# A graph-attention megakernel: the adjacency ring of the attention loaded and counted by single blocks instead of five parts, with the first pair of units of each chunk written out ahead of its loop

## The chip, the core and the metric

The kernel runs on one core of a Trainium2 chip. The metric is the device time of one execution in microseconds (us). The core has five engines that run side by side and meet only at semaphores: TensorE (PE in the profile; its weight loads are PEld), VectorE (DVE), ScalarE (ACT), GpSimd (POOL) and SyncE (SP). SP computes nothing here; it issues all the DMA transfers of the kernel, one after the other, and waits in between for whatever each transfer needs.

## What is computed

Four graph layers run one after the other on x (3327 nodes, 128 features) and a dense adjacency matrix adj (3327 x 3327). Each layer is followed by a residual and a layer norm. Layers 0, 2 and 3 are graph convolutions of different kinds. The change lies in layer 1, an attention:

```
n, d = x.shape                      # 3327, 128
h = Wq.shape[0] // d                # 8
q = (x @ Wq.T).reshape(d, n, h)     # 128 "batches", each with 3327 rows of 8
k = (x @ Wk.T).reshape(d, n, h)
v = (x @ Wv.T).reshape(d, n, h)
a = einsum('dnh,dmh->dnm', q, k) * d ** -0.5
a = softmax(a + adj + adj, axis=2)  # adj is both spatial and edge encoding
out = einsum('dnm,dmh->dnh', a, v).reshape(n, h * d) @ Wo.T
```

So there are 128 batches of a 3327 x 3327 score matrix, and the same adjacency is added (twice) to each of them.

## The kernel before

**Chunks, units and blocks.** The 26 blocks of 128 query rows are split into four chunks, `CHUNKS = ((24, 2), (0, 8), (8, 8), (16, 8))` (first block, number of blocks). Chunk 0 has only two query blocks, and four batches are done side by side in it; chunks 1 to 3 have eight query blocks (1024 columns) and one batch at a time. One such piece of work is a *unit*: 32 units in chunk 0 and 128 in each of the others, 416 in all. A unit goes over the 26 key blocks j = 0 to 25, each a tile of 128 keys by 1024 query columns. All loops are over pairs of units (`Fori`), whose bodies are written out in full.

**What happens to a block.** TensorE computes the scores (L1097) into PSUM. For 18 of the blocks VectorE adds the adjacency (L1209, `added`) and ScalarE takes the exponential of two or three such blocks at once (L1170). For the other 8, `POOL_BLOCKS = (0, 3, 6, 9, 13, 16, 19, 22)`, ScalarE takes the exponential first (L1167) and GpSimd multiplies it by a prepared factor exp(2 adj) (L1183, `multiplied`). TensorE then weighs V with the result (L1117), some five to seven blocks later, and at block 9 of the next unit VectorE copies the finished sums out (`finish`, L1194). TensorE scores up to four blocks ahead; VectorE's blocks have two score places, GpSimd's one.

**The ring.** The adjacency (or factor) block j of a chunk has to lie in SBUF for all units of the chunk: 26 blocks of 128 x 1024 floats, 512 KB each (128 KB each in chunk 0). The ring `adj_ring` has 28 slots of a full block, `ADJ_SLOTS = BLOCKS + 2`. In chunks 1 to 3, block j of the next chunk goes into the slot that block j - 2 of this chunk has, and blocks 0 and 1 into the two spare slots. Chunk 0's small blocks lie from slot 21 on, and some of its keys in slots 13 to 20.

**Loading and counting by parts.** `ADJ_PARTS` cuts the 26 blocks into five parts, 0 to 5, 6 to 12, 13 to 16, 17 to 20 and 21 to 25, with one semaphore each (`ring.loaded[part]`). VectorE (L1203 to L1205) and GpSimd (L1180, L1181) wait at the first block of a part until all of the part has landed. They do this in every pair of units, as the wait stands in the loop's body. GpSimd waits only at those first blocks that are its own, 0 and 13.

**The changeover on SP.** Inside a chunk SP loads, per unit, keys and queries (`load`, L630, L637, L975), V (`load_v`, L984) and stores the sums (`store`, L1005). When a chunk c from 1 on ends, SP's order is: once the last unit but one is scored, `load(c + 1, 0, 0)` (keys and queries of the next chunk's first unit); five waits that the present chunk's ring has landed; `used`, which waits until the last unit has done block 3; ring part 0; V of the next chunk's first unit; a store; parts 1, 2 and 3, each behind a `used`; once the last unit is scored, keys and queries of the next chunk's second unit; part 4; its V; the last store. From chunk 0 to chunk 1 there is room for parts 0 and 1 already during chunk 0; part 2 comes when the last unit but one is scored, and parts 3 and 4, then the second unit's keys and queries, when the last one is.

Of the kernel before, what the change touches and what calls it, by code (L numbers as in the profile page):

```python
# [13 lines left out]
ALU = mybir.AluOpType  # L14
# [731 lines left out]
def bound_phase(nc, keep, q_norms, k_norms, top, flag, ring, k_tile):  # L746
# [3 lines left out]
    with ExitStack() as stack:  # L750
# [9 lines left out]
        @block.sync  # L760
        def _(sp):
            sp.dma_start(k_len[:, :], k_norms[0:BATCHES * N].rearrange("(d n) -> d n", n=N)).then_inc(k_loaded, LOAD)
            sp.dma_start(q_len[:, :], q_norms[0:BATCHES * N].rearrange("(d n) -> d n", n=N)).then_inc(q_loaded, LOAD)
            for part in range(len(ADJ_PARTS)):
                ring.load(sp, 0, part, True)
# [67 lines left out]
class AdjRing:  # L833
# [4 lines left out]
    def __init__(self, mem, adj_t, factors):  # L838
        self.adj_t, self.factors = adj_t, factors
        self.tile = mem.sb("adj_ring", [P, ADJ_SLOTS * WIDTH])  # L840
        self.loaded = mem.sems("adj_ring_loaded", len(ADJ_PARTS))
        self.part_of = [n for n, (begin, end) in enumerate(ADJ_PARTS) for _ in range(begin, end)]
# [7 lines left out]
    def load(self, sp, c, part, factored):  # L850
        first, nb = CHUNKS[c]
        for j in range(*ADJ_PARTS[part]):
            of = self.adj_t[first:first + nb, :, j, :]
            if factored and j in POOL_BLOCKS:
                of = self.factors[first:first + nb, :, POOL_BLOCKS.index(j), :]
            sp.dma_start(self.block(c, j).rearrange("p (i q) -> p i q", q=P), of.rearrange("i p q -> p i q")
                         ).then_inc(self.loaded[part], LOAD)

    def ready(self, c, part, factored):

        times = c + 1 if factored else c + 2
        return times * (ADJ_PARTS[part][1] - ADJ_PARTS[part][0]) * LOAD


def attention_phase(nc, keep, ring, k_tile, pool_blocks, k_parts, q_parts, q_shift, v_ext, o_rows):
# [45 lines left out]
    with ExitStack() as stack:  # L911
# [49 lines left out]
        def _(sp):  # L961
# [45 lines left out]
            def next_part(c, part):  # L1007
                ring.load(sp, c + 1, part, n_pool > 0)
# [4 lines left out]
            for part in range(len(ADJ_PARTS)):  # L1013
                sp.wait_ge(ring.loaded[part], ring.ready(0, part, True))
                if not n_pool:
                    ring.load(sp, 0, part, False)
                    sp.wait_ge(ring.loaded[part], ring.ready(0, part, False))
            for part in range(2):
                next_part(0, part)
            spare = ADJ_SLOTS - BLOCKS  # L1020
            for c in range(len(CHUNKS)):
# [16 lines left out]
                if more:  # L1038
                    all_scored(done - 1)
                    load(c + 1, 0, 0)  # L1040
                    if c:
                        for part in range(len(ADJ_PARTS)):
# [130 lines left out]
        def _(pool):  # L1173
            if n_pool:
# [580 lines left out]
```

## Time and profile before

| | |
|---|---|
| time of the runs | 11077.53 us (median of 3, 11073.33 to 11080.54) |
| span of the profiled execution | 11077.6 us; no other time is given for it |
| busy share in the span | ScalarE 93%, TensorE 90%, VectorE 89%, GpSimd 72% |
| mean granted TensorE clock | 0.982 of full |
| attention | first add at 713.1 us, last at 10526.7 us |
| changes of chunk | about 1490, 4484 and 7512 us |
| loads of the ring | 104, of which 26 in the small form |

The times in rows are microseconds from the start of the span, unless marked ns. In a timeline, a row with xN stands for N instructions of one kind in a row, the second number is the time from the start of the first to the end of the last, and the square brackets hold the idle time of the engine before it and what ended it. For a DMA on SP's queue the second number is the time that the issue took; the landing, when all its data is in place, comes later and is listed by itself as microseconds from issue to landing (least, median, most). PEclk is TensorE's granted clock as a share of the full 2.4 GHz. TensorE's busy time is modelled.

### The profile page before, as it was taken

The numbers are of one execution on the slowest core, as the hardware profiler recorded it, in microseconds if no ns is written. First come the engines' busy times: TensorE is split into PE (matmuls) and PEld (weight loads), VectorE is DVE, ScalarE is ACT, GpSimd is POOL, SyncE is SP. The second block draws the span as 40 slices with busy tenths as digits, with TensorE's granted clock in tenths as the row PEclk, the third lists the DMA queues.
The fourth block names the chain that finished last, engine by engine and source line by source line (L and its number), as shares of the span: only waits on it lengthen the run. The fifth ranks groups of instructions, "written<-read, shape, count | busy, mean of one in ns | idle before, by whom it ended". The sixth has DMA issues, their size and how long they took to land. (4 is left out here: it accounts for less than half of the span.)

```text
span 11077.6 us, 307002 instructions
## 1 busy us (share of the span) xinstructions
PE 9989.2 (90%) x115286; PEld 4513.5 (41%) x115286; DVE 9834.5 (89%) x9022; ACT 10277.8 (93%) x7161; POOL 7988.9 (72%) x3346
## 2 busy tenths in 40 slices
PE   5859999999999999899999999998999999999988
PEld 5525543333333333333333333333333333333383
DVE  7469989999999999899999999998999999999958
ACT  3559999999999999999999999999999999999916
POOL 0038878888888888788888888887888888888800
PEclk8979999999999999999999999999999999999999
DMA  9997743333333332433333333335332333333264
GB/s 389 319 226 101 100 84 50 50 49 48 48 50 50 50 49 48 94 50 49 48 48 50 50 50 49 48 48 95 50 49 48 49 50 50 49 49 47 46 209 176
DMA packets 426842, 902.84 MB, mean 82 GB/s; under 512 B 86887, under 2 KB 349038, under 8 KB 379790
## 3 DMA queue, kind: packets, MB, share of 16 engines
q1 hardware_dynamic: 426732, 901.33, 40.5%
q8 instruction: 74, 1.21, 0.0%
q14 instruction: 36, 0.29, 0.0%
HBM read 745.35 MB, written 155.64 MB: 81 GB/s over the span
## 5 line engine op out<-in xcount | busy, mean ns | idle before, releaser
L1209 DVE SCALAR_TENSOR_TENSOR a_probs<-ps,adj_ring 128x1024 f32<-128x1024 f32 x7488 | 8855.1, 1220 | 777.3 <-PE ps L1097 633.4
L1183 POOL TENSOR_TENSOR a_pool_probs<-a_pool_probs,adj_ring 128x1024 f32<-128x1024 f32 x3328 | 7972.6, 2396 | 1884.3 <-ACT a_pool_probs L1167 1877.7
L1170 ACT ACTIVATE a_probs<-a_probs 128x2048 f32<-128x2048 f32 (+1 forms) x3328 | 8701.1, 2615 | 42.9 <-DVE a_probs L1209 42.7
L1167 ACT ACTIVATE a_pool_probs<-ps 128x1024 f32<-128x1024 f32 x3328 | 5012.0, 1506 | 49.1 <-PE ps L1097 49.1
L1097 PE MATMUL ps<-a_q,a_k 34*128 34x512 f32 (+1 forms) x21632 | 4091.5, 445 | 806.5 <-ACT a_pool_probs L1167 614.6
L1117 PE MATMUL ps<-a_probs,a_v 128*9 128x256 f32 x59904 | 3860.2, 380 | 0.0
L1097 PEld LDWEIGHTS ps<-a_q,a_k 34*128 34x128 f32 x21632 | 1794.5, 185 | 3477.0 <-ACT a_pool_probs L1167 1631.1
L1117 PEld LDWEIGHTS ps<-a_probs,a_v 128*9 128x9 f32 x59904 | 1579.3, 91 | 1602.0 <-issue 201.4
L1117 PE MATMUL ps<-a_pool_probs,a_v 128*9 128x256 f32 x26624 | 2068.1, 382 | 1.5 <-POOL a_pool_probs L1183 1.5
L1117 PEld LDWEIGHTS ps<-a_pool_probs,a_v 128*9 128x9 f32 x26624 | 395.4, 88 | 974.2 <-issue 937.6
L602 POOL MEMSET v_rows<- 128x512 f32 x2 | 1.9, 1038 | 403.6 <-POOLq L90 403.6
L1097 PE MATMUL ps<-a_q,adj_ring 34*128 34x256 f32 x1664 | 222.4, 280 | 0.0
L1627 POOL MEMSET e_nat<- 128x1 f32 x3 | 0.2, 98 | 300.3 <-POOLq L90 300.3
L1194 DVE COPY a_o<-ps 128x256 f32<-128x256 f32 x417 | 177.0, 424 | 30.1 <-PE ps L1117 5.2
L296 ACT ACTIVATE tr<-ps 128x1664 f32<-128x1664 f32 x52 | 78.4, 1555 | 134.2 <-DMA adj_t<-tr 124.3
L272 PE MATMUL ps<-ident,nat 128*128 128x128 f32 x676 | 108.2, 334 | 99.2 <-ACT tr L296 91.4
L796 POOL MEMSET a_k<- 128x3328 f32 x2 | 5.7, 2872 | 245.4 <-POOLq L90 245.4
L416 PE MATMUL ps<-g0z,g0tile 128*128 128x128 f32 x1352 | 155.7, 277 | 9.4 <-DVE g0z L467 9.4
L1097 PEld LDWEIGHTS ps<-a_q,adj_ring 34*128 34x128 f32 x1664 | 161.1, 190 | 0.0
L1590 PE MATMUL ps<-e_both,e_h 128*128 128x512 f32 (+2 forms) x364 | 152.1, 569 | 7.1 <-DVE e_both L1650 7.1
L416 PEld LDWEIGHTS ps<-g0z,g0tile 128*128 128x128 f32 x1352 | 154.4, 194 | 9.5 <-issue 9.5
L1445 PE MATMUL ps<-g2z,g2tile 128*128 128x128 f32 x1352 | 155.1, 277 | 1.3 <-PEq L90 1.3
(174 smaller groups left out, 2177.6 us busy)
## 6 DMA issues: line engine op xcount, KB each, us to landing
a_k<-k_parts SPq DMA_DIRECT2D x1664, 208.0 KB
a_q<-q_parts SPq DMA_DIRECT2D x3072, 16.0 KB
a_v<-v_ext SPq DMA_DIRECT2D x384, 117.0 KB, 2.1
adj_t<-tr SPq DMA_DIRECT2D x26, 1664.0 KB, 20.7
g0tile<-adj_t SPq DMA_DIRECT2D x26, 1664.0 KB, 9.6
g2tile<-adj_t SPq DMA_DIRECT2D x26, 1664.0 KB
nat<-in_adj SPq DMA_DIRECT2D x25, 1663.5 KB, 18.8
e_nat<-in_adj SPq DMA_DIRECT2D x25, 1663.5 KB, 7.0
```

Of the source, the lines that this page charges most:

```text
L272: ins = nc.tensor.transpose(ps[:, col:col + P], nat[b][:, P * j:P * (j + 1)], keep.ident[:, :])
L296: nc.scalar.activation(tr[b][:, HALF * P * h:HALF * P * (h + 1)], ps[:, half * h:half * h + HALF * P], ACT.Copy).then_inc(copied[h], 1)
L416: ins = nc.tensor.matmul(acc[i % ACC_BUFS], layer.tile[b][:, j, :], z[:, j, :], start=j == 0, stop=j == BLOCKS - 1)
L1097: ins = nc.tensor.matmul(ps[:, at:at + half], keys[b][n][row:row + SCORE_ROWS, P * j:P * (j + 1)].bitcast(F32R), q_tile[b][row:row + SCORE ...
L1117: ins = nc.tensor.matmul(acc[b][32 * g:32 * g + VG, :], v_tile[b][0:rows_of[j], 3 - g if several else 0, j, :], p[:, SHARE * g:SHARE * (g ...
L1167: nc.scalar.activation(probs(k), score(j), ACT.Exp, scale=SCALE).then_inc(scores_exped, 1)
L1170: nc.scalar.activation(sums_of(k), sums_of(k), ACT.Exp, scale=2.0).then_inc(sums_exped, 1)
L1183: nc.gpsimd.tensor_tensor(beside(c, probs(k)), beside(c, probs(k)), adj_of(c, j), ALU.mult).then_inc(multiplied, 1)
L1194: v.tensor_copy(o_tile[b][:, :], acc[b]).then_inc(acc_read, 1)
L1209: v.scalar_tensor_tensor(out=beside(c, probs(k)), in0=beside(c, score(j)), scalar=SCALE / 2, in1=adj_of(c, j), op0=ALU.mult, op1=ALU.add). ...
L1445: ins = nc.tensor.matmul(acc[i % ACC_BUFS], second.tile[b][:, j, :], second.z[:, j, :], start=j == 0, stop=j == BLOCKS - 1)
L1590: ins = nc.tensor.matmul(ps[:, at:to], h[0:rows, i, :], both[i % 2][0:rows, at:to], start=begin and to < NP, stop=end, skip_group_check=True)
```

## The change

Ring blocks are loaded, counted and waited for one by one. There are 26 semaphores in place of five. `next_blocks(c, js)` issues blocks one at a time and, from chunk 1 on, puts before block j a wait that block j - 2 of the last unit is done (`used(c, j - spare)`, now one wait, on the engine that works on that block); blocks 0 and 1 have no such wait. The cuts in SP's order are moved: 13 blocks (in place of 6) before V of the next chunk's first unit, and 24 (in place of 21) before the keys and queries of its second unit. VectorE and GpSimd wait for each of their blocks in the first unit of a chunk only; for that the first pair of units of each chunk is written out ahead of the loop, and the loop has no waits for the ring. In the changeover from chunk 0 the order of the transfers is as before.

```diff
-ADJ_PARTS = ((0, 6), (6, 13), (13, 17), (17, 21), (21, BLOCKS))
+VALUES_FROM, KEYS_FROM = 13, 24
...
-        self.loaded = mem.sems("adj_ring_loaded", len(ADJ_PARTS))
+        self.loaded = mem.sems("adj_ring_loaded", BLOCKS)
...
-            def used(c, upto):
-                j, done = upto - 1, units_before[c + 1] - 1
-                sp.wait_ge(added, done * n_dve + dve_rank[j] + (not by_pool[j]))
-                if n_pool:
-                    sp.wait_ge(multiplied, done * n_pool + pool_rank[j] + by_pool[j])
+            def used(c, j):
+                done = units_before[c + 1] - 1
+                if by_pool[j]:
+                    sp.wait_ge(multiplied, done * n_pool + pool_rank[j] + 1)
+                else:
+                    sp.wait_ge(added, done * n_dve + dve_rank[j] + 1)
...
-            def next_part(c, part):
-                ring.load(sp, c + 1, part, n_pool > 0)
+            def next_blocks(c, js):
+                for j in js:
+                    if c and j >= spare:
+                        used(c, j - spare)
+                    ring.load(sp, c + 1, j, n_pool > 0)
...
                     if c:
-                        for part in range(len(ADJ_PARTS)):
-                            sp.wait_ge(ring.loaded[part], ring.ready(c, part, n_pool > 0))
-                        used(c, ADJ_PARTS[0][1] - spare)
-                        next_part(c, 0)
+                        for j in range(BLOCKS):
+                            sp.wait_ge(ring.loaded[j], ring.ready(c, n_pool > 0))
+                        next_blocks(c, range(VALUES_FROM))
                     else:
-                        next_part(c, 2)
+                        next_blocks(c, range(*KEYS_AT))
                     sp.wait_ge(batch_summed, done - 1)
                     load_v(c + 1, v_of_unit(c + 1, 0), 0)
                 sp.wait_ge(stored[1], (done // 2 - 1) * per_store)
                 store(c, done, last - 1, 0)
                 if more:
                     if c:
-                        for part in (1, 2, 3):
-                            used(c, ADJ_PARTS[part][1] - spare)
-                            next_part(c, part)
-                    all_scored(done)
-                    if c:
+                        next_blocks(c, range(VALUES_FROM, KEYS_FROM))
+                        all_scored(done)
                         load(c + 1, 1, 1)
-                        used(c, ADJ_PARTS[4][1] - spare)
-                        next_part(c, 4)
+                        next_blocks(c, range(KEYS_FROM, BLOCKS))
                     else:
-                        next_part(c, 3)
-                        used(c, BLOCKS)
-                        next_part(c, 4)
+                        all_scored(done)
+                        next_blocks(c, range(KEYS_AT[1], FEW_AT))
+                        if n_pool:
+                            used(c, pool_blocks[-1])
+                        used(c, BLOCKS - 1)
+                        next_blocks(c, range(FEW_AT, BLOCKS))
                         load(c + 1, 1, 1)
...
+            def add(c, pair, first):
+                for k in range(units):
+                    b, j = divmod(k, BLOCKS)
+                    unit = pair * 2 + b
+                    if not by_pool[j]:
+                        if first and b == 0:
+                            dve.wait_ge(ring.loaded[j], ring.ready(c, n_pool > 0))
...
-                with dve.Fori(units_before[c] // 2, units_before[c + 1] // 2) as pair:
...
+                begin, end = units_before[c] // 2, units_before[c + 1] // 2
+                add(c, begin, True)
+                with dve.Fori(begin + 1, end) as pair:
+                    add(c, pair, False)
```

GpSimd's `multiply(c, pair, first)` is built in the same way around L1183.

## Rows read from the trace of the kernel before

**Rows 1.** Busy time by stretch: us, engines' busy us (instructions), PEclk, DMA share, GB/s.

```profile
1550.00:4400.00 2850.00, 2648.72 (x31638) 1093.91 (x31634) 2642.90 (x2314) 2850.00 (x1948) 2332.22 (x974) 1.00 0.31 49
1490.00:1516.00 26.00, 22.05 (x202) 8.63 (x196) 16.67 (x15) 18.96 (x13) 15.40 (x7) 0.74 0.48 72
4484.00:4540.00 56.00, 35.18 (x298) 13.26 (x294) 26.35 (x25) 28.55 (x19) 22.48 (x10) 0.70 0.86 184
7512.00:7564.00 52.00, 30.94 (x292) 11.62 (x292) 26.05 (x24) 25.80 (x18) 20.11 (x10) 0.77 0.92 189
```

**Rows 2.** VectorE's timeline, chunk 1 to 2: start, us, engine, line, operands [idle before].

```profile
4437.38 0.42 DVE L1194 COPY a_o<-ps 128x256 f32<-128x256 f32 x1
...
4449.70 8.41 DVE L1209 SCALAR_TENSOR_TENSOR a_probs<-ps,adj_ring 128x1024 f32<-128x1024 f32 x7 [0.69 <-PE ps L1097]
...
4460.80 0.42 DVE L1194 COPY a_o<-ps 128x256 f32<-128x256 f32 x1
...
4521.53 3.49 DVE L1209 SCALAR_TENSOR_TENSOR a_probs<-ps,adj_ring 128x1024 f32<-128x1024 f32 x3 [9.63 <-DMA adj_ring<-adj_t]
...
4537.18 0.41 DVE L1194 COPY a_o<-ps 128x256 f32<-128x256 f32 x1
```

**Rows 3.** Landings of ring loads issued at 4506.08 (first), 4512.7 and 4514.5.

```profile
DMA to landing us min/median/max: 9.6/9.6/9.6
...
L856 SPq DMA_DIRECT2D adj_ring<-adj_t x2: 1639/1680/1720, 4512.7 to 4514.5; - x2
...
DMA to landing us min/median/max: 6.9/7.0/7.0
```

**Rows 4.** The sync queue's timeline, chunk 1 to 2.

```profile
4456.79 0.26 SPq L975 DMA_DIRECT2D a_q<-q_shift  x1
4462.81 0.39 SPq L856 DMA_DIRECT2D adj_ring<-factors  x1
...
4470.49 1.73 SPq L984 DMA_DIRECT2D a_v<-v_ext  x1
```

**Rows 5.** GpSimd's timeline, last unit of chunk 1.

```profile
4460.33 2.39 POOL L1183 TENSOR_TENSOR a_pool_probs<-a_pool_probs,adj_ring 128x1024 f32<-128x1024 f32 x1 [0.31 <-ACT a_pool_probs L1167]
```

**Rows 6.** Busy time by stretch, just before the ring's loads.

```profile
4458.50:4459.00 0.50, 0.50 (x10) 0.18 (x2) 0.50 (x1) 0.50 (x2) 0.50 (x1) 1.00 0.01 0
```

**Rows 7.** The sync queue's timeline at the start of attention.

```profile
715.53 0.40 SPq L986 DMA_DIRECT2D a_v<-v_ext  x1
716.11 0.39 SPq L856 DMA_DIRECT2D adj_ring<-factors  x1
```

**Rows 8.** The sync queue's and VectorE's timelines, chunk 2 to 3.

```profile
7483.24 0.25 SPq L975 DMA_DIRECT2D a_q<-q_shift  x1
7489.27 0.39 SPq L856 DMA_DIRECT2D adj_ring<-factors  x1
...
7547.48 3.49 DVE L1209 SCALAR_TENSOR_TENSOR a_probs<-ps,adj_ring 128x1024 f32<-128x1024 f32 x3 [12.14 <-DMA adj_ring<-adj_t]
...
7561.17 0.42 DVE L1194 COPY a_o<-ps 128x256 f32<-128x256 f32 x1
```

**Rows 9.** Busy time by stretch, a restart (the last figures are clock, DMA, GB/s).

```profile
1494.00:1506.00 12.00, 11.43 (x86) 4.21 (x86) 7.48 (x7) 8.21 (x5) 4.81 (x3) 0.50 0.58 87
```

**Rows 10.** VectorE's timeline, few-blocks chunk to chunk 1.

```profile
1488.01 1.23 DVE L1209 SCALAR_TENSOR_TENSOR a_probs<-ps,adj_ring 128x1024 f32<-128x1024 f32 x1 [0.26 <-PE ps L1097]
1493.29 3.48 DVE L1209 SCALAR_TENSOR_TENSOR a_probs<-ps,adj_ring 128x1024 f32<-128x1024 f32 x3 [4.05 <-DMA adj_ring<-adj_t]
...
1510.72 0.41 DVE L1194 COPY a_o<-ps 128x256 f32<-128x256 f32 x1
```

**Rows 11.** Landings of ring loads issued at 1479.3 and 1481.1.

```profile
DMA to landing us min/median/max: 8.5/10.3/12.0
```

**Rows 12.** DMA issues of the page: count, KB each, median us to landing.

```profile
a_v<-v_ext SPq DMA_DIRECT2D x384, 117.0 KB, 2.1
```

**Rows 13.** DMA queues from 4600 to 7400: packets, MB, share.

```profile
q1 hardware_dynamic: 57576, 137.57, 31.4%
```

More of the change, by code:

```diff
@@ L848, in block, with load, ready @@
         return self.tile[:, at:at + width]
-    def load(self, sp, c, part, factored):
+    def load(self, sp, c, j, factored):
         first, nb = CHUNKS[c]
[L852 to L862, printed above, removed]
+        of = self.adj_t[first:first + nb, :, j, :]
+        if factored and j in POOL_BLOCKS:
+            of = self.factors[first:first + nb, :, POOL_BLOCKS.index(j), :]
+        sp.dma_start(self.block(c, j).rearrange("p (i q) -> p i q", q=P), of.rearrange("i p q -> p i q")
+                     ).then_inc(self.loaded[j], LOAD)
+    def ready(self, c, factored):
+        return (c + 1 if factored else c + 2) * LOAD
 def attention_phase(nc, keep, ring, k_tile, pool_blocks, k_parts, q_parts, q_shift, v_ext, o_rows):
@@ L1012, in _ @@
                 load_v(0, v_of_unit(0, b), b)
-            for part in range(len(ADJ_PARTS)):
-                sp.wait_ge(ring.loaded[part], ring.ready(0, part, True))
+            for j in range(BLOCKS):
+                sp.wait_ge(ring.loaded[j], ring.ready(0, True))
                 if not n_pool:
[L1016 to L1019, printed above, removed]
+                    ring.load(sp, 0, j, False)
+                    sp.wait_ge(ring.loaded[j], ring.ready(0, False))
             spare = ADJ_SLOTS - BLOCKS
+            next_blocks(0, range(KEYS_AT[0]))
             for c in range(len(CHUNKS)):
@@ L1194, in finish @@
                 v.tensor_copy(o_tile[b][:, :], acc[b]).then_inc(acc_read, 1)
+            def add(c, pair, first):
+                for k in range(units):
+                    b, j = divmod(k, BLOCKS)
+                    unit = pair * 2 + b
+                    if not by_pool[j]:
+                        if first and b == 0:
+                            dve.wait_ge(ring.loaded[j], ring.ready(c, n_pool > 0))
+                        dve.wait_ge(scores_ready[False], unit * n_dve + (dve_rank[j] + 1))
+                        v.scalar_tensor_tensor(
+                            out=beside(c, probs(k)), in0=beside(c, score(j)), scalar=SCALE / 2, in1=adj_of(c, j),
+                            op0=ALU.mult, op1=ALU.add).then_inc(added, 1)
+                    if j == FINISH_AT:
+                        finish(1 - b, unit)
             v.memset(ps[:, BANK * 6:], 1.0).then_inc(cleared, 1)
@@ L1198, in _ @@
             for c in range(len(CHUNKS)):
-                with dve.Fori(units_before[c] // 2, units_before[c + 1] // 2) as pair:
-                    for k in range(units):
-                        b, j = divmod(k, BLOCKS)
-                        unit = pair * 2 + b
-                        if b == 0 and j in (begin for begin, _ in ADJ_PARTS):
-                            part = ring.part_of[j]
-                            dve.wait_ge(ring.loaded[part], ring.ready(c, part, n_pool > 0))
-                        if not by_pool[j]:
-                            dve.wait_ge(scores_ready[False], unit * n_dve + (dve_rank[j] + 1))
-                            v.scalar_tensor_tensor(
-                                out=beside(c, probs(k)), in0=beside(c, score(j)), scalar=SCALE / 2, in1=adj_of(c, j),
-                                op0=ALU.mult, op1=ALU.add).then_inc(added, 1)
-                        if j == FINISH_AT:
-                            finish(1 - b, unit)
+                begin, end = units_before[c] // 2, units_before[c + 1] // 2
+                add(c, begin, True)
+                with dve.Fori(begin + 1, end) as pair:
+                    add(c, pair, False)
             dve.wait_ge(stored[1], (units_before[-1] // 2 - 1) * per_store)
```

23 lines of the change are left out of this document (11 added, 12 removed).

## The prediction

> **What bounds the kernel now.** I read the views in this order: busy time by stretch, the timelines of VectorE, GpSimd and the sync queue around the three changes of chunk, and the landings of the ring's loads. The reader is to see first that inside a chunk ScalarE is busy without a gap [rows 1]: it sets the pace, and one unit takes 4460.80 - 4437.38 = 23.42 us from one copy of the sums (L1194) to the next [rows 2]. Speeding another engine up there changes nothing. Time is lost only where a chunk ends. There ScalarE is idle for 26 - 18.96 = 7.0 us (few-blocks chunk to chunk 1), 56 - 28.55 = 27.5 us (1 to 2) and 52 - 25.80 = 26.2 us (2 to 3) [rows 1]. These 60.7 us, 0.55% of the span, are all that the change can work on.
>
> Why they are lost: 26 blocks of 512 KB have to arrive, and with the queue full SP gets rid of one only every 4514.5 - 4512.7 = 1.8 us [rows 3], while a unit uses one every 23.42 / 26 = 0.90 us. Two ring slots are spare; every other load waits until the last unit has freed a slot. So the end of a changeover is set by the landing of the last block, plus what must be done after it.
>
> **Where the ring's loads start.** Before, SP is through with the next chunk's keys and queries at 4456.79 + 0.26 = 4457.05, then sits until 4462.81 [rows 4]: it waits for block 3 of the last unit, the GpSimd multiply that starts at 4460.33 and runs 2.39 us [rows 5]. Meanwhile the DMA engines fall to nothing [rows 6]. After, blocks 0 and 1 need no slot of that unit. SP first passes 26 waits in place of 5. Five such waits cost it 716.11 - 715.53 - 0.40 = 0.18 us at the start of attention [rows 7], 0.036 us each, so 26 cost 0.9 us: first issue at 4458.0. Block 2 waits for block 0's multiply, which ended at 4460.33 - 0.31 = 4460.02 [rows 5]; the two blocks ahead of it keep the engines busy for 3.6 us, so they do not run dry. Block 5 waits for block 3 (4462.7), and its turn at that pace comes only at about 4467. Start shift: 4462.81 - 4458.0 = 4.8 us. From 2 to 3 it is the same: 7483.24 + 0.25 + 0.9 = 7484.4 against 7489.27, 4.9 us [rows 8]. Bounds: 5.7 if the waits cost nothing; 0 if the loads only pile up behind each other.
>
> **Where they end.** The same bytes go through the same queue. Before, unit 1's keys and queries go behind block 20; after, behind block 23. The second issue behind them (block 22 before, at 4506.08) lands 9.6 us later [rows 3]. After, that place is block 25's, 3 x 1.8 = 5.4 us later for the three blocks put ahead and 4.8 us earlier for the start: issued 4506.7, landed 4516.3. Before, block 25 was issued at 4514.5 and landed 6.9 us later, at 4521.4 [rows 3]. So the last landing moves 5.1 us earlier from 1 to 2; I take 4.9 from 2 to 3 (7547.4, just ahead of VectorE's start at 7547.48 [rows 8], becomes 7542.5).
>
> **What is left after it.** Before, VectorE could not touch block 21 until all of blocks 21 to 25 had landed; then it had blocks 21, 23, 24, 25 and six of the next unit to do before the copy. After, only 25 and those six. In the steady stretch add 21 starts at 4449.70 - 0.69 - 1.22 = 4447.8 and add 25 at 4452.1 [rows 2]: to the copy at 4460.80 that is 13.0 and 8.7 us. So 4.3 us of work move ahead of the last landing, into time in which VectorE idled. The restart is not at steady pace, as TensorE comes back at a granted clock of 0.50, 1.2 GHz [rows 9]. From VectorE's start on block 21 to the copy it took 15.6 us (4521.53 to 4537.18) [rows 2], 13.7 us (7547.48 to 7561.17) [rows 8] and 17.4 us (1493.29 to 1510.72) [rows 10]: 2.6, 0.7 and 4.4 us over 13.0, on average 2.6. After, VectorE works block by block, but keys and queries still hold it up for some 5 us just ahead of block 24, so the clock can fall again. I take the average, 2.6. Lower bound 0. Upper bound, all at the low level: TensorE's matmuls fill 2648.72 / 2850 of the time at full clock [rows 1], 0.84 us a block. The seven scorings to the copy need 5.9 us at full and 11.8 at half clock, with 2.7 for the first weighing and 1.0 for the last add 15.5 in all: 6.8 over the 8.7.
>
> A page bears on this. The Trainium skill, "TensorE: Matmul & The Clock Gate", section "Part 1: The HAM clock gate", holds that TensorE is throttled by default and that activity releases it. The trace agrees: 0.50 in the restarts. By that rule a changeover whose holes are short would keep 2.4 GHz, and the 2.6 us would go; the sum would be 5.2 us better.
>
> **Sum.** 1 to 2: the copy comes at 4516.3 + 8.7 + 2.6 = 4527.6 instead of 4537.18: 9.6 us. 2 to 3: 7542.5 + 11.3 = 7553.8 instead of 7561.17: 7.4 us. Few blocks to chunk 1: there the loads are issued in the same order at the same times. VectorE stood still from 1488.01 + 1.23 = 1489.24 to 1493.29 before block 21 [rows 10], for block 25 alone, issued at 1481.1 and landed 12.0 us later; block 24 had landed at 1479.3 + 8.5 = 1487.8 [rows 11]. After, it does 21, 23, 24 and wants 25 at 1492.9: 0.4 us of stall and no cold restart. Of ScalarE's 7.0 us I leave 0.8: 6.2 us gained (bounds 3 and 7.0). Start of attention: 21 more waits on SP, 0.8 us, ahead of a queue that soon is full; I charge 0.3 us (0 to 0.8).
>
> At no cost: the waits gone from VectorE's and GpSimd's loops (ScalarE has no gap there). V of the new chunk's first unit goes behind 13 blocks in place of 6: seven blocks are 12.7 us and the start 4.8 less, so it is issued at 4470.49 + 7.9 = 4478.4 [rows 4] and, at the 6.9 us of a ring load, there by 4485.3; TensorE wants it at about 4460.80 + 23.42 = 4484.2. What it loses is hidden by the wait for the blocks past 15; without that cover it would be 1 to 2 us. The store behind it is wanted only a unit later. The 21 added semaphores are cleared with the others at the phase's end. The longer straight code has to be loaded: today's chunk heads show no hole on VectorE but for the ring and TensorE [rows 2].
>
> 9.6 + 7.4 + 6.2 - 0.3 = 22.9 us. The profiled execution's span is 11077.6 us, with nothing listed around it, and the median of the runs is 11077.53, the same. Forecast: 11077.6 - 22.9 = 11054.7 us, 0.21% less.
>
> **Rivals.**
> A, *the drain takes the start back*: the last landing is no earlier, because keys and queries hold the queue up for longer when three more blocks are ahead of them. Left: 4.5 and 2.5 us of tail, 6.2 and -0.3: 12.9 us, 11064.7. For it: a block right behind them needs 9.6 us where another needs 6.9 [rows 3]. Against: the engines stand empty before the ring's loads today [rows 6], and the bytes are the same. Chance 0.15.
> B, *cold to the copy*: TensorE stays at 1.2 GHz all the way, 4.2 us more in each of two restarts: 14.5 us gained, 11063.1. For it: it stayed there for 12 us in one restart [rows 9]. Against: in the shortest it cost 0.7 us in all. Chance 0.14.
> C, *never cold*: work block by block keeps the clock up, 2.6 us less twice, and the full 5.7 us of start: 29.9 us, 11047.7. It is what the page above would give. Against: the hole before block 24. Chance 0.12.
> D, *slower: loops that fetch their code again*: the pair in front moves each loop body of VectorE and GpSimd to another address. If one body lay so that each pass had to fetch, the 63 passes of a chunk would each pay a transfer, 2.1 us as V's in quiet stretches [rows 12], less VectorE's slack of 2 x 0.7 us a pair (ScalarE's 23.42 against 18 x 1.22 + 0.42 + 0.3): 63 x 0.7 = 44 us, 11099 with the rest as summed. It decides from 22.9 / 63 = 0.36 us a pass. Against: today 2800 us of looping show no packet but the kernel's own queue's [rows 13]. The Trainium skill, "Runtime: NRT & Kernel Launch", section "Instruction fetch mechanics", says that a taken branch to a place outside the fetched pages forces a fetch first; by the same rows no loop here does so yet. Chance 0.04.
>
> **How the numbers follow.** My sum has 0.55. Its own range, from the restart (0.7 to 4.4 each) and the start (3 to 5.7), is 11049 to 11062. A and B reach to 11065, C to 11048, A and B together to 11073. Range 11046 to 11069: D and the worst combination stay outside, under 2 in 10. A difference of 0.2% (22 us) is about what can be told from no change. That line is 11055.4, so close to the forecast that the sum falls on its faster side 6 times in 10, 0.33; with C 0.12 and 0.03 for gains I do not see, 0.48. Slower by over 0.2%: 0.04. The rest, 0.48, is within.
>
> **What the new profile would show.** Right: ring loads issued about 1 us after the queries of the next chunk, no empty DMA stretch there; VectorE's waits for the ring split into short ones from about block 15 on; ScalarE idle about 1, 18 and 19 us in place of 7.0, 27.5 and 26.2; 23.42 us a unit elsewhere. Wrong: a last landing at the old distance from the old chunk's end (A); over 5 us lost between add 25 and the steady pace (B); none lost (C); instruction packets or a longer unit inside a chunk (D); TensorE waiting for a_v or a_q, the moved transfers not hidden.

## The result, and the profile after

The changed kernel takes 11060.68 us (median of 20 runs, 11054.0 to 11069.0) against 11077.7 us (20 runs, 11070.68 to 11081.78): the ratio is 0.9986, with a 95% interval of 0.9979 to 0.9992. That is 17.0 us less where 22.9 were forecast, inside the range, and by 0.14% on the "within 0.2%" side of the line. The profiled execution has a span of 11062.8 us, 14.8 less than that of before. The attention starts 1.75 us later in it (first add at 714.83 instead of 713.08) and is itself about 17 us shorter, from that add to its last copy of the sums.

One correction to the text on the kernel before: GpSimd's waits for the ring stand at blocks 0, 6 and 13, as block 6 too is its own and the first of a part. No number hangs on it.

Busy time by stretch comes first, for the same places as in [rows 1], shifted by as much as the last unit's copy has moved (+1.26, -0.98 and -6.66 us); then the steady stretch. Columns are as there.

```profile
1491.26:1517.26 26.00, 22.91 (x230) 9.02 (x222) 18.30 (x17) 20.62 (x14) 16.67 (x7) 0.80 0.46 74
4483.02:4539.02 56.00, 40.03 (x360) 15.16 (x356) 30.40 (x28) 33.77 (x23) 26.42 (x12) 0.73 0.82 167
7505.34:7557.34 52.00, 37.09 (x380) 14.41 (x384) 31.09 (x28) 34.27 (x24) 26.83 (x12) 0.80 0.84 171
...
1550.00:4400.00 2850.00, 2648.76 (x31640) 1093.70 (x31642) 2644.31 (x2314) 2850.00 (x1948) 2330.29 (x974) 1.00 0.31 49
```

ScalarE's idle time is now 5.4, 22.2 and 17.7 us in place of 7.0, 27.5 and 26.2 [rows 1]; forecast were about 1, 18 and 19. That is 1.7, 5.2 and 8.5 us less in place of about 6, 9.5 and 7. The steady stretch is what it was, to 0.04 us of TensorE: nothing was gained or lost inside a chunk. So the reading of where the time can be was right, and the first changeover is where the forecast missed by most.

VectorE's timeline, chunk 1 to 2 in the kernel after (it answers to [rows 2]):

```profile
4459.82 0.42 DVE L1197 COPY a_o<-ps 128x256 f32<-128x256 f32 x1
...
4483.23 0.42 DVE L1197 COPY a_o<-ps 128x256 f32<-128x256 f32 x1
...
4499.41 1.23 DVE L1207 SCALAR_TENSOR_TENSOR a_probs<-ps,adj_ring 128x1024 f32<-128x1024 f32 x1 [2.39 <-DMA adj_ring<-adj_t]
4501.23 1.23 DVE L1207 SCALAR_TENSOR_TENSOR a_probs<-ps,adj_ring 128x1024 f32<-128x1024 f32 x1 [0.59 <-DMA adj_ring<-adj_t]
4506.89 1.23 DVE L1207 SCALAR_TENSOR_TENSOR a_probs<-ps,adj_ring 128x1024 f32<-128x1024 f32 x1 [4.43 <-DMA adj_ring<-adj_t]
4515.75 1.23 DVE L1207 SCALAR_TENSOR_TENSOR a_probs<-ps,adj_ring 128x1024 f32<-128x1024 f32 x1 [7.64 <-DMA adj_ring<-adj_t]
4517.38 2.36 DVE L1207 SCALAR_TENSOR_TENSOR a_probs<-ps,adj_ring 128x1024 f32<-128x1024 f32 x2 [0.41 <-DMA adj_ring<-adj_t]
...
4530.59 0.42 DVE L1197 COPY a_o<-ps 128x256 f32<-128x256 f32 x1 [1.29 <-PE ps L1115]
```

Before, VectorE waited once for five blocks; now it works each block as it lands (4499.41 to 4506.89), stands still for the hole that the second unit's keys and queries tear (7.64 us before block 24 at 4515.75), and has only block 25 (4517.38) and what follows ahead of the copy. Measured from the old unit's copy (4460.80 before, 4459.82 now), VectorE gets its last block 57.6 us later, against 60.7 before. Forecast was a landing 5.1 us earlier; it is 3.2.

The sync queue in the same place (it answers to [rows 4]), and under it how long after issue the first ring load, and blocks 24 and 25, landed:

```profile
4455.82 0.25 SPq L972 DMA_DIRECT2D a_q<-q_shift  x1
4456.93 0.40 SPq L854 DMA_DIRECT2D adj_ring<-factors  x1
...
4505.98 0.25 SPq L972 DMA_DIRECT2D a_q<-q_shift  x1
4506.28 1.02 SPq L854 DMA_DIRECT2D adj_ring<-adj_t  x2
```

```profile
DMA to landing us min/median/max: 5.7/5.7/5.7
...
DMA to landing us min/median/max: 9.4/10.0/10.6
```

The 26 waits take 4456.93 - 4455.82 - 0.25 = 0.86 us (0.9 forecast), and the ring starts 4.90 us earlier against the old unit's copy (4.8 forecast). But block 0 now lands 5.7 us after its issue. Before, on empty engines, it was 4.1:

```profile
L856 SPq DMA_DIRECT2D adj_ring<-factors x1: 393/393/393, 4462.8 to 4462.8; - x1
...
DMA to landing us min/median/max: 4.1/4.1/4.1
```

The engines move 128 GB/s in 4457 to 4461, just behind the keys and queries, and 282 once the ring has them to itself. The reading is that the tail of the keys and queries is still arriving. It fits all the rows at hand: 5.7 us in the other changeover of this kernel too (issued at 7477.7), and 4.1 us again in experiment 4 for a first ring load that goes out ahead of the keys (at 4439.1).

```profile
4457.00:4461.00 4.00, 4.00 (x52) 1.59 (x52) 3.47 (x5) 4.00 (x4) 3.68 (x2) 1.00 0.88 128
...
4459.00:4483.00 24.00, 22.34 (x276) 9.14 (x268) 22.24 (x20) 24.00 (x18) 19.32 (x10) 1.00 1.21 282
```

Few-blocks chunk to chunk 1, VectorE and then TensorE (it answers to [rows 10]):

```profile
1492.40 3.61 DVE L1207 SCALAR_TENSOR_TENSOR a_probs<-ps,adj_ring 128x1024 f32<-128x1024 f32 x3 [0.69 <-PE ps L1095]
1498.15 1.23 DVE L1207 SCALAR_TENSOR_TENSOR a_probs<-ps,adj_ring 128x1024 f32<-128x1024 f32 x1 [2.14 <-PE ps L1095]
...
1509.82 0.42 DVE L1197 COPY a_o<-ps 128x256 f32<-128x256 f32 x1 [1.27 <-PE ps L1115]
```

```profile
1493.93 0.73 PE L1095 MATMUL ps<-a_q,a_k 34*128 34x512 f32 x4
1497.61 0.50 PE L1095 MATMUL ps<-a_q,a_k 34*128 34x512 f32 x2 [2.94 <-DMA a_q<-q_shift]
```

The wait for the ring is gone, as forecast. In its place TensorE waits 2.94 us for the second unit's keys and queries, which stand behind block 25 in the queue. It comes back at 2.4 GHz, falls to 1.2 GHz within two microseconds, and works at that without a gap until about 1509.5:

```profile
1498.00:1499.00 1.00, 1.00 (x22) 0.53 (x24) 0.85 (x1) 1.00 (x1) 1.00 (x1) 1.00 0.00 0
1499.00:1500.00 1.00, 1.00 (x14) 0.34 (x8) 0.37 (x1) 0.25 (x1) 0.11 (x1) 0.58 0.78 200
...
1499.50:1509.00 9.50, 9.50 (x70) 3.54 (x70) 5.94 (x5) 5.65 (x4) 4.74 (x2) 0.50 0.69 104
```

**What is added up below.** The *excess* of a changeover is the sum of the distances from copy to copy across it, less 23.42 us each. Before it was 7.8, 28.8 and 27.1 us; after, 5.8, 23.4 and 18.7. The *restart* is the time from VectorE's start on block 25 to the copy in that unit; in the steady stretch it is 8.7 us. Both are read from one profile of each kernel; the clock, as will be seen, moves them by some us from one changeover to the next.

### The profile page after: what moved, and what is told of

The parts are those of the page before. It is cut to its first block and busy times, and to the rows that moved or that the text cites. A ratio compares the mean times of both kernels' runs of the same rounds, so it can differ in the third digit from the quotient of the medians.

```text
span 11062.8 us, 306459 instructions
## 1 busy us (share of the span) xinstructions
PE 9991.2 (90%) x115286; PEld 4517.4 (41%) x115286; DVE 9840.4 (89%) x9022; ACT 10276.4 (93%) x7161; POOL 7981.3 (72%) x3346
```

## The experiments

Nine kernels. Each is set against runs of the kernel before on the same chip: 11077.54 us for the first four, 11074.91 for the next four and 11074.31 for the last. Each differs from the kernel after by what its diff shows, except the second, which starts from the kernel before.

**1. The waits alone.** The cuts and the gate of before are put back; blocks are loaded and waited for one by one.

```diff
-VALUES_FROM, KEYS_FROM = 13, 24
+VALUES_FROM, KEYS_FROM = 6, 21
...
+                        used(c, 3)
                         next_blocks(c, range(VALUES_FROM))
```

> The changed kernel with the order and the gate of before: ring loads start behind block 3 of the last unit, V behind block 5, the second unit's keys behind block 20; only the counting and waiting are by single blocks. Theory (two separate parts: the start of the loads moves the last landing, the waits move 4.3 us of adds ahead of it): last landing as before (60.6 us after the old chunk's last copy from 1 to 2, 60.2 from 2 to 3), changeovers 2 to 4 us shorter each from 1 to 2 and 2 to 3, and 2.0 us from chunk 0 to 1 as in the changed kernel; in all 6 to 10 us less than before, 11068 to 11072. Rival (the single waits are the whole gain): as the changed kernel, 11061. Rival (the waits gain nothing without the start): 11076 to 11078.

Measured: 11066.39 us (11059.69 to 11078.7), ratio 0.9990 [0.9981, 0.9999]: 11.1 us faster than before. Excess 3.8, 21.8 and 22.7. VectorE gets block 25 60.4 and 60.5 us after the old copy, as before (60.7, 60.2): without the early start the last landing does not move. This kernel's gain lies behind that landing: 4.3 us of adds in each of two changeovers are done ahead of it. Its profile is of the fastest of its runs (11059.69) and shows more than that, as its restart from 1 to 2, 8.2 us, is 3.1 us nearer to the steady pace than it was before.

**2. The early start alone.** From the kernel before: part 0 is cut in two, and its first two blocks need no slot.

```diff
-ADJ_PARTS = ((0, 6), (6, 13), (13, 17), (17, 21), (21, BLOCKS))
+ADJ_PARTS = ((0, 2), (2, 6), (6, 13), (13, 17), (17, 21), (21, BLOCKS))
...
-                        used(c, ADJ_PARTS[0][1] - spare)
                         next_part(c, 0)
+                        used(c, ADJ_PARTS[1][1] - spare)
+                        next_part(c, 1)
```

> The kernel before with its first part cut into blocks 0 and 1 (issued at once) and 2 to 5 (behind block 3's use); waits by part everywhere. Theory: the last landing moves 3 us earlier in the changeovers 1 to 2 and 2 to 3, as in the changed kernel (it moved 3.1 and 3.3 there), the adds behind it stay; 6 us less than before, 11071 to 11073, nothing from chunk 0 to 1. Rival (the start gains nothing, the gates hold the later blocks up): 11077 to 11079.

Measured: 11073.25 us (11062.51 to 11077.97), ratio 0.9995 [0.9986, 1.0004]. By itself the early start is worth 4.3 us, and the interval takes in nothing. The profile says more: VectorE's last ring wait ends 56.7 and 56.1 us after the old copy, 4.0 and 4.2 earlier than before. So rival A is wrong, the start is not taken back in the drain. But its 8.2 us in the landings are not all seen in the median, and this profile is of the fastest of the kernel's runs (11062.51). It also has an excess of only 4.5 us from chunk 0 to 1, where this kernel does just what the kernel before does and that had 7.8: VectorE waits for block 25 in both (3.78 and 4.05 us), but TensorE then runs at 1.2 GHz for 3.4 us here and for 13.7 there. Together the two parts give 11.1 + 4.3 = 15.4 of the 17.0 us.

**3. The cuts of before.** All of the change, but with V and the second unit's keys where they were.

```diff
-VALUES_FROM, KEYS_FROM = 13, 24
+VALUES_FROM, KEYS_FROM = 6, 21
```

> The changed kernel with V behind block 5 and the second unit's keys and queries behind block 20, as before. Theory (bytes are conserved, the place of the keys only moves the hole): last landing within 1 us of the changed kernel's, time within 3 us of it, 11058 to 11064. Rival (the hole just before block 24 is what lets TensorE's clock fall): the restart costs under 1 us in both, 4 to 6 us less than the changed kernel, 11055 to 11057. Rival (the later cuts are what gained): 5 us more, 11066.

Measured: 11058.6 us (11056.03 to 11066.63), ratio 0.9985 [0.9976, 0.9994]: 18.9 us faster than before. Excess 5.3, 19.0 and 19.9; block 25 at 57.2 and 56.9. The moved cuts bring nothing that can be told from zero.

**4. The spare blocks first.** The waits and blocks 0 and 1 go ahead of the next chunk's first keys.

```diff
-                    all_scored(done - 1)
-                    load(c + 1, 0, 0)
                     if c:
                         for j in range(BLOCKS):
                             sp.wait_ge(ring.loaded[j], ring.ready(c, n_pool > 0))
-                        next_blocks(c, range(VALUES_FROM))
+                        next_blocks(c, range(spare))
+                    all_scored(done - 1)
+                    load(c + 1, 0, 0)
+                    if c:
+                        next_blocks(c, range(spare, VALUES_FROM))
```

> The changed kernel with ring blocks 0 and 1 (spare slots) and the 26 waits issued ahead of the next chunk's first keys and queries, in a stretch where the DMA engines are idle. Theory (the drain of 26 blocks is bound by bytes and ends the changeover): 2 x 1.8 us of transfer leave the drain and the loads no longer start into the tail of the keys; the last landing moves 4 to 5 us earlier in each of two changeovers, 8 to 10 us less than the changed kernel, 11051 to 11053. Rival (the gates on the last unit's blocks set the pace of the first loads): block 2's gate keeps the rest where it is, under 2 us less, 11059 to 11061.

Measured: 11056.22 us (11048.71 to 11057.88), ratio 0.9979 [0.9970, 0.9988]: 21.3 us faster than before. VectorE gets block 25 52.6 and 52.1 us after the old copy:

```profile
4459.05 0.42 DVE L1199 COPY a_o<-ps 128x256 f32<-128x256 f32 x1
...
4511.64 2.36 DVE L1209 SCALAR_TENSOR_TENSOR a_probs<-ps,adj_ring 128x1024 f32<-128x1024 f32 x2 [0.44 <-DMA adj_ring<-adj_t]
...
4523.15 0.41 DVE L1199 COPY a_o<-ps 128x256 f32<-128x256 f32 x1
```

That is 4.9 us earlier than in the kernel after (57.6), and 4.8 in the other changeover: 3.6 are the two blocks at 1.8 us, and the rest is near the 1.6 us of the overlap with the tail of the keys. What counts is how early the engines have ring loads to themselves. Of the 9.7 us the restarts took some back, 11.5 and 12.9 us to the copy against 8.7 at full pace, and the medians show 4.3 us more than for the kernel after.

**5. From the few-blocks chunk, slots one by one.** A small block of chunk 0 lies in a quarter of a slot; blocks 21 to 24 of chunk 1 are issued as soon as the four small ones in their slot are done, instead of behind the last unit's scores. The second unit's keys and queries, behind them, come earlier too.

```diff
+                        for n in range(4):
+                            few = range(4 * n, 4 * n + 4)
+                            used(c, max(j for j in few if not by_pool[j]))
+                            if n_pool:
+                                used(c, max(j for j in few if by_pool[j]))
+                            next_blocks(c, (FEW_AT + n,))
                         all_scored(done)
                         next_blocks(c, range(KEYS_AT[1], FEW_AT))
...
-                        next_blocks(c, range(FEW_AT, BLOCKS))
+                        next_blocks(c, (BLOCKS - 1,))
```

> The changed kernel; in the changeover from chunk 0 alone, blocks 21 to 24 of chunk 1 are issued slot by slot as the last unit of chunk 0 frees its small blocks, in the stretch before that unit is all scored, where the DMA engines are idle; 17 to 20, 25 and the keys follow as before. Theory (what was left of that changeover, 5.8 us over the steady pace, comes from the second unit's keys and queries, which TensorE waited for until 1497.6): four blocks of 1.8 us leave the queue ahead of them, they land about 7 us earlier and the wait of TensorE for a_q is gone; the changeover costs under 1 us over steady and the time is 4 to 6 us less than the changed kernel's, 11055 to 11057. Rival (the landing of block 25 or the gates on slots delay it all the same): changeover still 3 us or more, 11060.

Measured: 11054.78 us (11051.6 to 11060.24), ratio 0.9981 [0.9972, 0.9990]: 20.1 us faster than before. The changeover has gone; its excess is nil:

```profile
1475.60 2.20 SPq L630 DMA_DIRECT2D a_k<-k_parts  x2
```

The same load in the kernel after:

```profile
1485.50 2.18 SPq L630 DMA_DIRECT2D a_k<-k_parts  x2
```

VectorE's copies in this experiment:

```profile
1477.63 0.42 DVE L1203 COPY a_o<-ps 128x256 f32<-128x256 f32 x1
...
1501.05 0.42 DVE L1203 COPY a_o<-ps 128x256 f32<-128x256 f32 x1
...
1524.47 0.42 DVE L1203 COPY a_o<-ps 128x256 f32<-128x256 f32 x1
```

The second unit's keys start 2 us before the old unit's copy, where the kernel after starts them 5.5 us behind it (1485.50 against 1479.99). With them in time TensorE does not wait, and the clock stays: 1.00 in all of 1480 to 1530. The other two changeovers are as in the kernel after (18.9 and 21.1). By the medians, experiment 5 gains 3.1 us on the kernel after.

**6. Small keys.** In the last two changeovers the second unit of a new chunk loads only 128 columns of its keys; the rest of that buffer keeps old keys, so this unit computes something else and the kernel is a measurement only. This leaves out some 800 KB behind block 23.

```diff
-            def load(c, d, b):
+            def load(c, d, b, short=False):
...
-                        load_k(sp, k_to, row, k_of[batch], sem)
+                        if short:
+                            load_k(sp, k_to[:, 0:P], row, k_of[batch][:, 0:P], sem)
+                        else:
+                            load_k(sp, k_to, row, k_of[batch], sem)
...
-                        load(c + 1, 1, 1)
+                        load(c + 1, 1, 1, True)
```

> The changed kernel, but in the changeovers 1 to 2 and 2 to 3 the keys of the second unit are loaded for the first 128 of 3328 columns only (the same number of transfers, 32 KB in place of 832 KB; the rest of that unit's keys are left stale, so its part of the output is other work). Theory (the 8.9 us between the landings of blocks 23 and 24 are the keys' transfer, bound by their bytes on few rows): the hole shrinks to 2 to 4 us, the last landing moves 5 to 6 us earlier in each, 10 to 12 us less than the changed kernel, 11049 to 11051. Rival (the hole is SP's time to issue the 14 transfers, 6 us): the last landing moves by under 2 us, 11057 to 11061.

Measured: 11048.62 us (11044.07 to 11054.09), ratio 0.9976 [0.9965, 0.9986]. The hole shrinks but stays:

```profile
4504.51 1.22 DVE L1210 SCALAR_TENSOR_TENSOR a_probs<-ps,adj_ring 128x1024 f32<-128x1024 f32 x1 [2.97 <-DMA adj_ring<-adj_t]
4509.02 1.23 DVE L1210 SCALAR_TENSOR_TENSOR a_probs<-ps,adj_ring 128x1024 f32<-128x1024 f32 x1 [3.29 <-DMA adj_ring<-adj_t]
4510.82 2.36 DVE L1210 SCALAR_TENSOR_TENSOR a_probs<-ps,adj_ring 128x1024 f32<-128x1024 f32 x2 [0.57 <-DMA adj_ring<-adj_t]
```

From block 23 to block 24 it is 4.5 us in place of 8.9. Block 25 comes 51.9 us after the old copy in place of 57.6, and both restarts are short (9.4 and 9.5 us). 4.4 us for some 800 KB are about 180 GB/s, an estimate, against 282 for the ring; why these bytes cost more is not shown. Of the 4.5 us that are left, 1.8 are the ring block itself; the rest fits the issuing of the 14 transfers, which takes SP from 4498.70 to 4505.04.

**7. No pair in front.** The waits stand in the loops' bodies again.

```diff
-                    multiply(c, begin, True)
-                    with pool.Fori(begin + 1, end) as pair:
-                        multiply(c, pair, False)
+                    with pool.Fori(begin, end) as pair:
+                        multiply(c, pair, True)
...
-                add(c, begin, True)
-                with dve.Fori(begin + 1, end) as pair:
-                    add(c, pair, False)
+                with dve.Fori(begin, end) as pair:
+                    add(c, pair, True)
```

> The changed kernel without the pair in front: the waits by block stand in the loops, 18 on VectorE and 8 on GpSimd in each pair of units. Theory (ScalarE sets the pace inside a chunk and a passed wait costs some 0.04 us of a slack of 0.7 us a unit): 23.42 us a unit and the changed kernel's time within noise, 11058 to 11064. Rival (the pair in front is worth something, as 18 waits take VectorE's slack): 18 x 0.04 = 0.7 us a pair, just at the slack; if it were over it by 0.1 us a pair, 19 us more, 11080.

Measured: 11059.48 us (11057.03 to 11062.68), ratio 0.9986 [0.9977, 0.9995], the ratio of the kernel after. The pair in front is worth nothing and costs nothing.

**8. Both early starts, keys behind block 15.** Experiments 4 and 5 together, and the second unit's keys moved forward.

```diff
-VALUES_FROM, KEYS_FROM = 13, 24
+VALUES_FROM, KEYS_FROM = 13, 16
...
```

> The two early issues together (spare blocks ahead of the next chunk's first keys, and chunk 0's slots as they come free), and the second unit's keys behind block 15 in place of 23. Theory (the three changeovers are separate, bytes are conserved, and the hole that the keys make does no harm where it stands far from the last landing): 9 us as from the spare blocks alone, 5 us of the chunk 0 changeover, and a restart under 1 us over steady in place of 3 to 4: 11044 to 11049. Rival (with the hole moved, blocks 16 on come late and the clock falls there as well): restart unchanged, 11050 to 11053.

Measured: 11046.83 us (11039.77 to 11050.4), ratio 0.9973 [0.9962, 0.9983]: 28.1 us faster than before. Excess nil, 14.7 and 18.4. The same kernel shows both kinds of restart. In chunk 1 to 2 it took 9.2 us, in 2 to 3 12.9, with these rows of busy time by stretch, each from about where block 25 is added:

```profile
4510.00:4520.00 10.00, 9.72 (x122) 4.02 (x123) 9.66 (x10) 9.96 (x8) 7.18 (x3) 1.00 0.57 84
...
7520.00:7530.00 10.00, 10.00 (x74) 3.52 (x70) 6.39 (x6) 7.77 (x5) 4.61 (x2) 0.50 0.70 100
```

In the one TensorE is back at 2.4 GHz, in the other it works ten microseconds without a gap at 1.2 GHz.

**9. The same with the cut of after.** Only `KEYS_FROM` differs from 8: it is 24.

```diff
-VALUES_FROM, KEYS_FROM = 13, 16
+VALUES_FROM, KEYS_FROM = 13, 24
```

> The change with both early starts (26 waits and blocks 0 and 1 ahead of the next chunk's first keys; from chunk 0 on the small blocks 21 to 24 issued one by one as their slots come free), the cuts left at 13 and 24. It differs from the last kernel only in where the second unit's keys and queries stand: behind block 23, not behind block 15. Theory: the queue is bound by its bytes, so the last landing stays where it is, 52 to 53 us behind the old unit's copy; but the hole of some 8 us now stands just before block 24, so TensorE restarts at 1.2 GHz and the restart costs 2.8 to 4.2 us as in the kernel with the spare blocks first, where it cost about 0.5: some 3 us more in each of two changeovers, a median 5 us above 11046.8, with 11050 to 11054 as its range, and an excess of 16 to 18 us in each of the last two changeovers. Rival: where the hole stands is worth nothing and the run comes out within 2 us of 11046.8. Second rival: the last kernel loses something by the early keys (they wait for all scores of the old unit, and the ring behind them stops), and this one is 3 us or more faster than it.

Measured: 11048.24 us (11040.84 to 11056.72), ratio 0.9975 [0.9966, 0.9984]. It is 26.1 us faster than before, 8 is 28.1. The first rival is the nearest: by the medians the place of the hole is worth 2 us, which these intervals don't tell from nothing. In the two profiles the excess is 36.3 against 33.1 us over the last two changeovers, but the restarts are 13.2 and 11.5 here and 9.2 and 12.9 there, so they do not go with the place of the hole.

Beside each other (us; the difference is that of the medians, the excess is from one profile each; block 25 is counted from the old unit's copy; in 2 it is block 21, and it restarts from there, at 13.0 in the steady stretch):

| kernel | difference | excess 0-1, 1-2, 2-3 | block 25 | restart |
|---|---|---|---|---|
| after | -17.0 | 5.8, 23.4, 18.7 | 57.6, 56.9 | 13.2, 9.4 |
| 1 waits | -11.1 | 3.8, 21.8, 22.7 | 60.4, 60.5 | 8.2, 9.7 |
| 2 start | -4.3 | 4.5, 23.6, 23.0 | 56.7, 56.1 | 13.6, 13.8 |
| 3 old cuts | -18.9 | 5.3, 19.0, 19.9 | 57.2, 56.9 | 9.3, 10.6 |
| 4 spare first | -21.3 | 3.5, 16.5, 17.6 | 52.6, 52.1 | 11.5, 12.9 |
| 5 few slots | -20.1 | 0, 18.9, 21.1 | 57.2, 57.2 | 9.3, 11.5 |
| 6 small keys | -26.3 | 3.7, 13.7, 13.6 | 51.9, 51.7 | 9.4, 9.5 |
| 7 no pair | -15.4 | 4.9, 20.8, 19.6 | 56.8, 57.8 | 11.5, 9.5 |
| 8 both early | -28.1 | 0, 14.7, 18.4 | 53.1, 52.9 | 9.2, 12.9 |
| 9 both, cut 24 | -26.1 | 0, 19.8, 16.5 | 54.0, 52.5 | 13.2, 11.5 |

The last column goes with the clock. From VectorE's start on block 25, the granted clock is back at 2.4 GHz after 2.7 to 3.9 us wherever the restart is 9.2 to 9.7 us (experiment 2 aside, whose count starts at block 21), after 7.7 to 8.6 where it is 10.6 to 11.5, and after 12.2 to 12.8 where it is 12.9 to 13.2; in the one restart of 8.2 us it is back before. The excess from chunk 0 to 1 does the same. The kernel after and experiments 1, 3, 4, 6 and 7 have the same orders from chunk 0 to 1, and TensorE waits 2.9 to 3.6 us for the second unit's queries in all of them. Where it then runs at 1.2 GHz for 3.4 us the excess is 3.5 to 3.8 (1, 4 and 6), for 6.8 us it is 4.9 and 5.3 (7 and 3), and for 10.2 us 5.8 (after).

## Why the prediction was right, and where it was too high

**The bound.** Right. The steady stretch did not move, and all of the gain is in the changeovers.

**Start of the ring's loads.** Right: 4.90 and 4.92 us earlier against 4.8 and 4.9; 26 waits took 0.86 us.

**Last landing.** Right in kind, too large in size: the term of the sum that was mis-sized. It is 3.2 and 3.4 us earlier instead of 5.1 and 4.9. Two numbers explain the first. Block 25 was put on the queue at 4506.7, the time forecast, but the old unit's copy had moved 1.0 us forward, so it is 1.0 late in the frame of the changeover; and it landed 10.6 us after its issue, not 9.6. The first goes with block 0's 5.7 us instead of 4.1: with the early loads in the tail of the next chunk's first keys, up to 1.6 of the 4.9 us are spent before the ring runs at its pace. Why the second took 10.6 us no run settles. The forecast counted the stretch from issue to issue and took the engines to be free. Experiment 4, which puts those loads ahead of the keys, gets 4.8 to 4.9 us more; experiment 6 shows that the same queue is also shorter when bytes behind block 23 are left out. Rival A, that the drain takes all of it back, fell with this profile and with experiment 2, but about a third of the start is taken back.

**Work ahead of the last landing.** Right. Only block 25 and the next unit's six are left; with the landing where it was, experiment 1 is 11.1 us faster, against two times 4.3 and what the first changeover gives.

**The restart.** Forecast 2.6 us in each. In the kernel after it is 13.2 - 8.7 = 4.5 and 0.7 us, 2.6 on average, and over the six changeovers of the kernels after, 5 and 7, which run the same orders there, 2.0. That the average is just the forecast's 2.6 is luck, as its size is not fixed: rivals B (cold to the copy) and C (never cold) each describe single changeovers, not the kernel, and B was priced too high, at 6.8 us where a restart that is cold almost to the copy costs 4.5. Experiment 8 has 0.5 and 4.2 in one execution. What the rows show is that the clock falls twice, once well before the hole and once in it. In the kernel after, chunk 1 to 2:

```profile
4484.00:4492.00 8.00, 6.65 (x88) 2.96 (x88) 5.96 (x5) 7.97 (x7) 6.03 (x4) 1.00 1.20 296
4492.00:4494.00 2.00, 0.43 (x4) 0.07 (x2) 0.01 (x1) 2.00 (x2) 2.00 (x1) 1.00 1.22 290
4494.00:4496.00 2.00, 0.73 (x10) 0.30 (x10) 1.42 (x2) 0.55 (x1) 1.64 (x2) 1.00 1.22 290
4496.00:4498.00 2.00, 1.36 (x14) 0.42 (x10) 1.03 (x1) 0.94 (x1) 1.05 (x1) 0.51 1.22 290
...
4504.00:4506.00 2.00, 2.00 (x22) 0.56 (x14) 0.00 (x0) 0.40 (x1) 0.85 (x1) 0.50 1.29 167
4506.00:4508.00 2.00, 0.57 (x2) 0.19 (x2) 1.11 (x1) 1.02 (x1) 0.21 (x1) 0.93 0.79 110
4508.00:4510.00 2.00, 0.50 (x2) 0.19 (x2) 0.11 (x1) 0.00 (x0) 2.00 (x1) 0.93 1.11 147
4510.00:4512.00 2.00, 0.00 (x0) 0.00 (x0) 0.00 (x0) 0.00 (x0) 0.13 (x1) 0.50 0.98 104
...
4508.70:4517.00 8.30, 0.00 (x0) 0.00 (x0) 1.23 (x1) 0.00 (x0) 1.43 (x1) 0.56 1.00 171
4517.00:4529.00 12.00, 11.97 (x84) 4.33 (x88) 7.99 (x7) 8.41 (x5) 4.31 (x2) 0.50 0.57 84
```

Once the blocks come at the ring's pace, 1.8 us each, TensorE is busy for 1.16 of the 4 us up to 4496 and drops from 2.4 to 1.2 GHz; busy again, it is back at 2.4 from about 4506.3; and in the hole, in which it has no work, it drops once more at about 4510. After the hole it works without a gap at 1.2 GHz until about 4530. From 2 to 3 it goes the same way (down at 7517, back at 7527, down at 7530.5, back at 7541). So the restart begins at 1.2 GHz because of the second fall, and there the forecast's hole is borne out; the fall ahead of it, at the pace of the ring, the forecast did not have. Why one restart has the clock back after some 4 us and the next after 13, with TensorE busy without a gap in both, is open: neither the place of the hole (experiment 9) nor its length (7.6 and 7.5 us on VectorE in the two changeovers of the kernel after) sets it. The Trainium skill, "TensorE: Matmul & The Clock Gate", section "Part 1: The HAM clock gate", has activity raise the clock; the trace agrees in direction, and the steady stretch at 1.00 and experiment 5 with it. It does not rise at once: in the last of the rows above TensorE is busy for 11.97 of 12.00 us at 0.50. No run shows a changeover that is paced by the ring and stays warm.

**Few-blocks chunk to chunk 1.** This step failed. The prediction had VectorE wait for block 25 "for block 25 alone", and after the change "0.4 us of stall and no cold restart", 6.2 us gained. The gain is 2.0 by the two profiles, and even that leans on the clock: at 3.4 us of 1.2 GHz the excess is 4.5 with the waits by parts (experiment 2) and 3.5 to 3.8 with single waits, so that what the waits alone gave here is an estimated 1 us. The next thing late, 3 us behind block 25, was the load that stands behind it in the queue: the second unit's keys and queries, for which TensorE waited 2.94 us; it then worked at 1.2 GHz from about 1499 almost to the copy at 1509.82. "TensorE waiting for a_v or a_q" stood among the forecast's own signs of being wrong, though for transfers that the change moves, and these it does not move. The prediction followed the ring's semaphores to the end of their list and stopped there. Experiment 5, which brings these transfers forward, has no excess left at that place. It moves ring blocks forward too, but VectorE does not wait for the ring there in the kernel after, so the late keys and queries are the cause, and all of the 3.5 to 5.8 us could be had.

**What was costed at nothing.** Right: V of the first unit (issued at 4478.75) lets nothing wait (copy at 4483.23, 23.41 us after the last), the removed waits in the loops and the pair in front are worth nothing (experiment 7), the start of the attention shows no loss (first add to the copy at 1478.73 before and 1479.99 after: 765.65 and 765.16 us).

**Sum.** Landings and tails gave 5.6 and 7.7 us to the first new copy where 9.6 and 7.4 were forecast, the first changeover 2.0 instead of 6.2: 15.3 where 23.2 were forecast. The medians give 17.0; the other 1.8 us of the attention in this profile cannot be placed, as chunk 0 alone takes 762.6 to 768.8 us in the profiles of this study.

**Rival D**, loops that fetch their code again. Refuted: a unit takes 23.42 us as before, from 4600 to 7400 the kernel after shows no packets but the kernel's own queue's, and experiment 7, without the pair in front, takes the same time.

```profile
q1 hardware_dynamic: 57377, 136.88, 31.0%
```

## What to carry to other kernels

Where a changeover is bound by a queue, count its bytes from the moment the engines are free for them, not from the first issue: the start moved 4.9 us and the end 3.2 to 3.4, and two blocks sent ahead of the keys brought 4.9 more. When a wait goes, ask for each transfer behind it in the same queue when it lands and who wants it; the next unit's keys, 3 us behind the last block, took back most of what it could have given. When two profiles differ by a few us, look at how long each worked at 1.2 GHz before calling it the change. Waits block by block pay (11 us here) only because an engine can then work while the queue drains; that needs no unrolled pair ahead of the loop.

## What the runs showed that was not expected

- A ring load issued right behind the key and query loads lands after 5.7 us instead of 4.1.
- Key loads are slow per byte: some 800 KB less are 4.4 us less, an estimated 180 GB/s, where the ring's loads reach 282 to 296.
- TensorE's clock leaves 2.4 GHz already where the ring's pace leaves it little work, some 12 us before it stands still, comes back, and falls again in the hole. A restart then costs between nothing and 4.5 us over the steady pace, and within one execution 0.7 and 4.5, by how long the clock stays at 1.2 GHz. That may be much of the 15 us between the runs of the kernel after, but no run shows it.
- The fastest version that computes the same, experiment 8, is 28.1 us faster than before: 11 us more than the change gave, from the order of the transfers alone.
